# A three-layer graph kernel on one core: the self edge taken out of the gathered edge lists

## The chip, the cores and the metric

The kernel runs on one core of a Trainium2 chip. The metric is the device time of one launch in microseconds, lower is better. PE is TensorE, DVE is VectorE, ACT is ScalarE, POOL is GpSimd, SP is SyncE.

## The reference, cut to what matters

The graph has n = 3125 nodes with D = 128 features, 103125 directed edges sorted by destination, 16 edge types (R), 4 attention heads (H) of 32 features (DH), and L = 3 layers. Two sets of 50000 edges are drawn, and behind them one edge from every node to itself; the sort by destination is stable.

```
_loop = jnp.arange(3125)
src = jnp.concatenate([_s, _d, _loop]); dst = jnp.concatenate([_d, _s, _loop])
_o = jnp.argsort(dst, stable=True); src = src[_o]; dst = dst[_o]
for l in range(3):
    ht = einsum('nd,rdo->nro', h, W_rel[l]);  msg = ht[src, etype]
    h_rel = segment_sum(msg, dst) + h @ W_loop[l] + b_rel[l]
    z = (h @ W_gat[l]).reshape(n, H, DH)
    e = leaky_relu(sum(z*attn_l)[src] + sum(z*attn_r)[dst], 0.2)
    alpha = softmax of e over the edges of one dst
    h_gat = segment_sum(alpha * z[src], dst) + b_gat[l]
    hc = concat([h_rel, h_gat]) @ W_fuse + b_fuse
    if l == 0: hc = hc * sigmoid(concat([hc, mean(weights)]) @ W_gate + b_gate)
    h = relu(hc)
out = layernorm(x + h)
```

So the last edge of every node's list is its edge to itself, with an edge type of its own.

## The kernel before, in words

**Table.** For each layer a table in HBM holds one row of 260 floats for every (node, edge type): 128 of the relation message and 132 of the attention (4 heads of 32 z and one logit). A padded list entry points at a null row (NULL) with a logit of -1e30. Two tables are used in turn.

**Setup.** Degrees are counted with matmuls, every node's edge list (`ell`, up to 80 row numbers) is gathered, nodes are ranked by degree, and POOL scatters (L561) each node's record of start, count, id, x and list in that order; the records come back as `meta`, 25 tiles of 128 nodes. Meanwhile PE, ACT and SP write the first layer's table (L441).

**One layer.** POOL, DVE, ACT and PE each run a loop over the 25 tiles of falling degree. POOL issues an indirect DMA (L594, `fetch`) per list position: 128 rows of 1040 bytes, one for each node. The number of positions of a tile is the largest degree in it (tile 0 is split in two half lists). They come in groups of 16 (PAIR): `H` first, into a buffer in the room of `meta_nat`, then `M1` (buffer in `late`) when there are 32 or more, and the rest, n mod 16, as the tail `T` (buffer in `scratch`). Read off the trace, the tiles have 29, 45, 42, 40, 39, 38, 37, 36, 36, 35, 35, 34, 33, 33, 32, 32, 31, 30, 30, 29, 28, 27, 26, 25 and 23 positions: 825 gathers in a layer. Tiles 1 to 15 have an M1 group, and all but 14 and 15 have a tail.

**What orders it.** Before H POOL waits for the list positions staged by DVE (`stage_head`) and for DVE to have finished the last H group (`free`); M1 and T have `stage_mid` and `stage_tail` likewise. `stage_tail` of a tile is written by `stage_this_tail` (L1344) at the start of that tile on DVE, behind two memsets of the tail buffer (L1334, L1335), and so behind the tail group and `end_tile` of the tile before. In layers 0 and 1 POOL also stores, after H of tile t, the finished table rows of tile t-2 for the next layer (L671, one scatter of 2 MB).

**DVE per tile.** `group` (L1346 on) adds the logits (`raw`, L1353), keeps a running maximum and rescales, sums messages (L1371), weights z by the exponentials that ACT makes (L788 to L1377), and sums (L1381). After the H group comes `epilogue` of the tile before: in layer 0 the gate, in layer 2 the norm. `end_tile` divides and hands `hr`, `hg` to PE (L1025), which transposes and fuses them; the result `hT` is multiplied by all 16 relation weights (L1049) for the next layer's rows, and ACT copies these into `rows` (`next_rows`, L816, L742, L819) and the next er and loop terms (h @ W_loop) into `meta`. At a layer's end POOL stores the last two tiles and waits for them before the first gather of the next (`s_stored`).

## Time and profile before, and how to read it

| | |
|---|---|
| median of 3 runs | 3485.82 us (3484.82 to 3485.93) |
| profiled execution: its span, first to last instruction | 3490.2 us (3490.178) |
| first layer's gathers | 214.5 to 1279 us |
| second layer's gathers | 1315.7 to 2381 us |
| third layer's gathers | 2411.8 to 3451.5 us |
| results stored | 3451.8 to 3484 us |
| POOL busy | 2489.3 us, 71% |
| DVE busy | 2380.3 us, 68% |

No separate time of the profiled execution is shown; its span alone is 4.4 us (0.13%) above the median of the runs. A busy share counts an instruction's own time; the gap between two gathers is called "issue", time in which the engine waited for nothing that the profile shows. A row of the timeline gives start, duration, engine, line and tile names, and in brackets the idle time before it and what ended that.

### The profile page before, as it was taken

Reading aid. Unit: us, or ns where it says so; the run is one execution under the profiler, and the core shown is the slowest. Engines: PE = TensorE matmul, PEld = TensorE weight load, DVE = VectorE, ACT = ScalarE, POOL = GpSimd, SP = SyncE. Lnnn points to the kernel's source line nnn. Section 1 sums busy time; section 2 is a strip of 40 time slices with the busy share of each in tenths; the row PEclk is TensorE's granted clock in tenths of the full one; section 3 lists DMA queues with packets and bytes.
Section 4 is the critical chain, followed back from the end, with each engine's and each line's share of the span. In section 5 each row is a group of like instructions: output and inputs, shape, how many; then the busy total and the mean of one; then the engine's idle time right before and its main releaser. Section 6 shows DMA issues by size and latency. Waiting matters only on the chain.

```text
span 3490.2 us, 18122 instructions
## 1 busy us (share of the span) xinstructions
PE 689.4 (20%) x1897; PEld 372.5 (11%) x1897; DVE 2380.3 (68%) x3226; ACT 424.8 (12%) x769; POOL 2489.3 (71%) x2642
## 2 busy tenths in 40 slices
PE   8942111222122230011121111221000000000000
PEld 5421000111011110000000000110000000000000
DVE  8536666677676764665777756674776788877786
ACT  3530110111111120101111111111000000000000
POOL 1457777777777756777777777775777777777776
PEclk9965555555655555555555555555555555555555
DMA  7774444455545544444454544454433333333332
GB/s 271 315 249 129 134 147 152 152 151 152 152 152 159 168 145 118 130 151 152 151 152 151 153 152 152 152 173 140 107 106 107 107 106 107 106 106 107 106 103 74
DMA packets 143244, 505.96 MB, mean 145 GB/s; under 512 B 44277, under 2 KB 51002, under 8 KB 133618
## 3 DMA queue, kind: packets, MB, share of 16 engines
q0 software_dynamic: 130032, 444.45, 43.4%
q1 hardware_dynamic: 13186, 61.24, 4.5%
q14 instruction: 19, 0.16, 0.0%
q8 instruction: 7, 0.11, 0.0%
HBM read 341.05 MB, written 164.51 MB: 145 GB/s over the span
## 4 chain that ended last, share of the span: by engine, by line
POOL 45%; issue 29%; DVE 10%; DMA 6%; PE 4%; POOLq 3%; DVEq 1%; ACT 1%; SPq 1%; ACTq 0%
POOL meta_nat L594 20%; POOL late L594 14%; POOL scratch L594 10%; DVE acc L1381 3%; PE ps_table L886 1%; DMA late<-table,stage_mid 1%; DMA table<-rows 1%; DMA scratch<-table,stage_tail 1%; DVE late L1377 1%; DVE scratch L1377 1%; DVE meta_nat L1377 1%; POOLq L369 1%; POOL table L671 1%; DMA meta_nat<-table,stage_head 1%; PE ps_cnt L919 1%
## 5 line engine op out<-in xcount | busy, mean ns | idle before, releaser
L594 POOL DMA_INDIRECT meta_nat<-table,stage_head x1200 | 1139.0, 949 | 395.7 <-issue 385.3
L594 POOL DMA_INDIRECT late<-table,stage_mid x720 | 681.9, 947 | 219.4 <-issue 217.9
L594 POOL DMA_INDIRECT scratch<-table,stage_tail x555 | 525.9, 948 | 175.5 <-issue 175.2
L1025 PE MATMUL ps_mix<-ident,hr 128*128 128x128 f32 x75 | 35.5, 473 | 1991.2 <-DVE hg L1401 1991.2
L788 ACT ACTIVATE ps_cnt<-logit 128x68 f32<-128x68 f32 x189 | 43.7, 231 | 2767.1 <-DVE logit L1363 2766.1
L1381 DVE TENSOR_REDUCE acc<-meta_nat 128x132 f32<-128x2112 f32 x75 | 290.6, 3875 | 8.1 <-DVE meta_nat L1377 0.5
L1371 DVE TENSOR_REDUCE acc<-meta_nat 128x128 f32<-128x2048 f32 x75 | 282.6, 3767 | 0.0
L1049 PE MATMUL ps_table<-wrel,hT 128*128 128x512 f32 x400 | 266.4, 828 | 0.0
L1353 DVE TENSOR_TENSOR raw<-late,er_cur 128x64 f32<-128x64 f32 x45 | 12.0, 267 | 324.5 <-DMA late<-table,stage_mid 324.5
L1025 PEld LDWEIGHTS ps_mix<-ident,hr 128*128 128x128 f32 x75 | 13.6, 182 | 2039.8 <-DVE hg L1401 2039.8
L1381 DVE TENSOR_REDUCE acc<-scratch 128x132 f32<-128x1188 f32 (+1 forms) x69 | 208.7, 3024 | 7.1
L1353 DVE TENSOR_TENSOR raw<-meta_nat,er_cur 128x64 f32<-128x64 f32 x75 | 20.1, 267 | 281.6 <-DMA meta_nat<-table,stage_head 280.2
L1371 DVE TENSOR_REDUCE acc<-scratch 128x128 f32<-128x1152 f32 (+1 forms) x69 | 204.9, 2970 | 8.8
L1381 DVE TENSOR_REDUCE acc<-late 128x132 f32<-128x2244 f32 x45 | 183.3, 4072 | 4.7
L1371 DVE TENSOR_REDUCE acc<-late 128x128 f32<-128x2176 f32 x45 | 178.2, 3961 | 5.5
L1334 DVE MEMSET scratch<- 128x1024 f32 (+1 forms) x75 | 93.0, 1240 | 125.5 <-issue 125.5
L1377 DVE TENSOR_TENSOR meta_nat<-meta_nat,ps_cnt 128x2112 f32<-128x2112 f32 x75 | 175.8, 2344 | 3.1 <-ACT ps_cnt L788 3.1
L742 ACT ACTIVATE rows<-ps_table 128x1024 f32<-128x1024 f32 x150 | 148.8, 1026 | 100.2 <-PE ps_table L886 62.4
L1049 PEld LDWEIGHTS ps_table<-wrel,hT 128*128 128x128 f32 x400 | 115.3, 288 | 136.6 <-issue 126.3
L1377 DVE TENSOR_TENSOR scratch<-scratch,ps_cnt 128x1188 f32<-128x1188 f32 (+1 forms) x69 | 127.2, 1843 | 0.0
L1377 DVE TENSOR_TENSOR late<-late,ps_cnt 128x2244 f32<-128x2244 f32 x45 | 111.7, 2482 | 0.0
L1031 PE MATMUL ps_mix<-hrT,wfuse 128*128 128x128 f32 x100 | 39.8, 501 | 363.6 <-ACT hgT L794 363.6
(237 smaller groups left out, 1701.4 us busy)
## 6 DMA issues: line engine op xcount, KB each, us to landing
table<-rows SPq DMA_DIRECT2D x25, 2080.0 KB, 7.7
meta_nat<-table,stage_head POOLq DMA_INDIRECT x1200, 2.8
late<-table,stage_mid POOLq DMA_INDIRECT x720
scratch<-table,stage_tail POOLq DMA_INDIRECT x555, 2.8
meta<-meta_ranked SPq DMA_DIRECT2D x1, 2438.0 KB, 15.1
wrel<-in_L_gnn_W_rel POOLq DMA_DIRECT2D x2, 1024.0 KB, 13.5
meta_nat<-in_x SPq DMA_DIRECT2D x1, 832.0 KB, 18.4
table<-rows,stage_id POOLq DMA_INDIRECT x50, 7.8
```

The costliest lines, as they stand in the source:

```text
L369: n = eng.value_load(tile_slots[0:1, bass.ds(t, 1)], min_val=PAIR, max_val=E)
L594: pool.indirect_dma_start(out=slots[b][:, k, :], out_offset=None, in_=table[l % 2], in_offset=bass.IndirectOffsetOnAxis(ap=index, axis=0)) ...
L671: pool.indirect_dma_start(out=table[(l + 1) % 2][0:NP_ * R, :].rearrange("(n r) f -> n (r f)", r=R), out_offset=bass.IndirectOffsetOnAxis( ...
L742: return s.activation(rows[k][:, j * R // 2:(j + 1) * R // 2, 0:D], ps_table[:, 1024 * j:1024 * j + 1024].rearrange("p (r f) -> p r f", f= ...
L788: s.activation(wgt[:, :, :, 0], logit[:], ACT.Exp).then_inc(s_wgt, 1)
L1025: pe.transpose(mix[0], hr[:], ident[:])
L1031: pe.matmul(mix[2], wfuse[:, 0], hrT[:], start=True, stop=False)
L1049: mm = pe.matmul(ps_table[:, 512 * c:512 * c + 512], hT[0][:], wrel[:, l + 1, c * RC * D:(c + 1) * RC * D], start=True, stop=True)
L1334: v.memset(messages("T", 1, slots_of_tail + 1), 0.0)
L1371: v.tensor_reduce(acc[:, 0:D], messages(b, lo, K + 1).rearrange("p k d -> p d k"), AX.X, ALU.add).then_inc(s_part, 1)
L1377: v.tensor_tensor(weighted(b, lo, K + 1), weighted(b, lo, K + 1), wgt[:, lo:K + 1].to_broadcast([P, K + 1 - lo, H, EX]), ALU.mult).then_in ...
L1381: v.tensor_reduce(acc[:, D:ROW], slots[b][:, lo:K + 1, D:ROW].rearrange("p k f -> p f k"), AX.X, ALU.add).then_inc(s_acc, 1)
```

## The change

Every node of tiles 1 to 24 (rank 128 and up) whose last edge is its own loses that list entry, and its count falls by one. The self edge's logit and z need no gather: in layers 1 and 2, ACT keeps each tile's z in `own_z` (in the room of `rows[1]`) when it writes the rows, and `start_tile` copies it into slot 0 of the H buffer, with `no_own` closing it for tile 0 and padding. Its relation message needs the row of its type: once `rows` of a tile stand, DVE multiplies all 16 rows by a one-hot mask of that type (`own_hot`), sums over the types and adds the sum to the loop term of the next layer (`add_own_messages`). The first layer has no such rows on chip, so it gathers the self edges as one more position, into slot 0 of H, for all 25 tiles. H groups take slot 0 in throughout. `yo` moves into the room of `wrel`.

```diff
+        own_z = rows[1][:].rearrange("p r f -> p (r f)")[:, 0:T * (D + H)].rearrange("p (t f) -> p t f", f=D + H)
...
+            def gather_head(l):
+                if l == 0:
+                    pool.indirect_dma_start(
+                        out=slots["H"][:, 0, :], out_offset=None, in_=table[l % 2],
+                        in_offset=bass.IndirectOffsetOnAxis(ap=stage_head[:, 0:1], axis=0)).then_inc(s_own_landed, 16)
+                gather(l, "H", stage_head[:, 1:PAIR + 1])
...
@@ ACT, next_rows and tile
                     act.wait_ge(s_stored, n_stored)
                     act.reg_add(n_stored, n_stored, 16)
+                    act.wait_ge(s_own_rows, n_own)
...
+                    s.activation(own_z[:, bass.ds(t, 1), :], ps_z[:, 0:D + H].rearrange("p (o f) -> p o f", o=1), ACT.Copy)
...
                 with act.If(groups > 1):
                     group()
-                    with act.If(groups > 2):
-                        group()
                 if not first:
                     next_rows(l, act.snap(n_last, min_val=0, max_val=T - 1))
                     act.reg_add(n_last, n_last, 1)
+                with act.If(groups > 2):
+                    group()
@@ DVE, setup
+            v.tensor_tensor(ell_valid, bc(iota_slot[:], T), bc_last(degree[:], ELL), ALU.is_lt)
+            step(v.tensor_scalar(last_at, degree[:], -1.0, None, ALU.add))
+            v.tensor_scalar(own_at, meta_nat[:, :, M_ID], float(R), 0.5 * (R - 1) - NULL, ALU.mult, ALU.add)
+            step(v.tensor_tensor(is_last, bc(iota_slot[:], T), bc_last(last_at, ELL), ALU.is_equal))
...
+                step(v.tensor_tensor(codes, lists, is_last[:, t0:t1], ALU.mult))
+                step(v.tensor_reduce(code, codes, AX.X, ALU.add))
+                step(v.tensor_tensor(gap, code, own_at[:, t0:t1], ALU.subtract))
+                step(v.tensor_tensor(gone, gap, gap, ALU.mult))
+                step(v.scalar_tensor_tensor(own, gone, 0.25 * R * R, may_drop[:, t0:t1], ALU.is_lt, ALU.mult))
+                step(v.tensor_tensor(gone, code, own, ALU.mult))
+                v.tensor_tensor(codes, is_last[:, t0:t1], bc_last(gone, ELL), ALU.mult)
+                step(v.tensor_tensor(degree[:, t0:t1], degree[:, t0:t1], own, ALU.subtract))
+                v.tensor_scalar(meta_nat[:, t0:t1, M_OWN], gone, float(NULL), None, ALU.add)
+                v.tensor_copy(meta_nat[:, t0:t1, M_CNT], degree[:, t0:t1])
+                v.scalar_tensor_tensor(lists, lists, float(NULL), codes, ALU.add, ALU.subtract).then_inc(s_ell_ok, 1)
@@ DVE, start_tile
+                else:
+                    z = own_z[:, bass.ds(t, 1), :].rearrange("p o (h e) -> p (o h) e", e=EX)
+                    v.tensor_copy(weighted("H", 0, 1)[:, 0, :, 0:DH], z[:, :, 0:DH])
+                    v.tensor_scalar(weighted("H", 0, 1)[:, 0, :, DH], z[:, :, DH], no_own[:, bass.ds(t, 1)], None, ALU.add)
...
+            def add_own_messages(l, t):
+                if l < L - 1:
+                    dve.wait_ge(s_rows, n_rows)
+                    dve.reg_add(n_rows, n_rows, 1)
+                    v.tensor_tensor(own_rows[:], rows[0][:, :, 0:D],
+                                    own_hot[:, bass.ds(t, 1), :].rearrange("p o (r f) -> p (o r) f", f=1
+                                                                           ).to_broadcast([P, R, D]), ALU.mult
+                                    ).then_inc(s_own_rows, 1)
+                    dve.wait_ge(s_own, n_own)
+                    dve.wait_ge(s_own_rows, n_masked)
+                    dve.reg_add(n_masked, n_masked, 1)
+                    v.tensor_reduce(own_sum[:], own_rows[:].rearrange("p r d -> p d r"), AX.X, ALU.add
+                                    ).then_inc(s_own_sum, 1)
+                    dve.wait_ge(s_own_sum, n_own)
+                    dve.reg_add(n_own, n_own, 1)
+                    loop = meta[:, bass.ds(t, 1), M_LOOP:META].rearrange("p o f -> p (o f)")
+                    v.tensor_tensor(loop, loop, own_sum[:], ALU.add).then_inc(s_own, 1)
...
@@ DVE, tile
                 with dve.If(in_first > 1):
                     group("M1")
+                    if not first:
+                        add_own_messages(l, dve.snap(n_last, min_val=0, max_val=T - 1))
...
                 if first:
                     merge_halves(l)
+                else:
+                    if l < L - 1:
+                        with dve.If(in_first < 2):
+                            add_own_messages(l, dve.snap(n_last, min_val=0, max_val=T - 1))
+                    dve.reg_add(n_last, n_last, 1)
                 end_tile(t)
```

Two places of the order of instructions. First DVE in the tile loop of layer 0, from the end of a short tail group (8 positions) to `hg`, the end of the tile. Before:

```order
L1381 TENSOR_REDUCE acc<-scratch 128x132
L1383 REGISTER_ALU
L1509 UNCONDITIONAL_BRANCH
L1396 RECIPROCAL rden<-acc 128x4
L1397 ISA
L1397 TENSOR_TENSOR hr<-acc,meta 128x128
```

Now:

```order
L1439 TENSOR_REDUCE acc<-scratch 128x132
L1441 REGISTER_ALU
L1596 UNCONDITIONAL_BRANCH
L1602 COMPARE_AND_BRANCH
L1475 ISA
L1476 TENSOR_TENSOR own_rows<-rows,own_hot 128x2048
L1482 REGISTER_ALU
L1483 TENSOR_REDUCE own_sum<-own_rows 128x128
L1486 ISA
L1488 TENSOR_TENSOR meta<-meta,own_sum 128x128
L1602 UNCONDITIONAL_BRANCH
L1458 RECIPROCAL rden<-acc 128x4
```

Three operations stand between the tail group's last sum and the end of the tile, for tiles without an M1 group; with one, the same three stand right behind the M1 group instead. Second ACT in the tile loop of layer 1, from the second group's exponentials to the rows of the tile before (`logit` to `ps_cnt` are the exponentials of one group). Before:

```order
L836 COMPARE_AND_BRANCH
L788 ACTIVATE ps_cnt<-logit 128x68
L789 REGISTER_ALU
L838 COMPARE_AND_BRANCH
L788 ACTIVATE ps_cnt<-logit 128x68
L789 REGISTER_ALU
L838 UNCONDITIONAL_BRANCH
L814 REGISTER_ALU
L816 ACTIVATE rows<-ps_z 128x16x132
```

Now:

```order
L868 COMPARE_AND_BRANCH
L816 ACTIVATE ps_cnt<-logit 128x68
L817 REGISTER_ALU
L868 UNCONDITIONAL_BRANCH
L842 REGISTER_ALU
L844 REGISTER_ALU
L846 ACTIVATE rows<-ps_z 128x16x132
L770 ACTIVATE rows<-ps_table 128x8x128 x2
L849 ISA
L849 ACTIVATE rows<-ps_z 128x132
```

The rows of the tile before are now made ahead of the third group's exponentials, and the copy into `own_z` follows them.

## Rows read from the trace of the kernel before

**Rows 1.** Page, part 1: busy time and share of each engine.
```profile
PE 689.4 (20%) x1897; PEld 372.5 (11%) x1897; DVE 2380.3 (68%) x3226; ACT 424.8 (12%) x769; POOL 2489.3 (71%) x2642
```
**Rows 2.** Groups by line: the gathers, busy and mean, idle before and its releasers.
```profile
L594 POOL DMA_INDIRECT meta_nat<-table,stage_head x1200 | 1139.0, 949 | 395.7 <-issue 385.3 <-DVE acc L1381 4.7 <-DVE stage_tail L1344 4.3
L594 POOL DMA_INDIRECT late<-table,stage_mid x720 | 681.9, 947 | 219.4 <-issue 217.9 <-DVE acc L1381 1.5
L594 POOL DMA_INDIRECT scratch<-table,stage_tail x555 | 525.9, 948 | 175.5 <-issue 175.2 <-DVE acc L1381 0.3
```
**Rows 3.** Timeline of POOL, second layer: last tail gather, store, next tail.
```profile
2246.51 0.95 POOL L594 DMA_INDIRECT scratch<-table,stage_tail  x1 [0.30 <-issue]
...
2267.81 1.00 POOL L671 DMA_INDIRECT table<-rows,stage_id  x1 [0.30 <-issue]
2269.11 0.97 POOL L594 DMA_INDIRECT scratch<-table,stage_tail  x1 [0.31 <-issue]
```
**Rows 4.** Timeline of DVE, second layer: a tail group, staging, a shorter tail's memset.
```profile
2249.37 0.26 DVE L1353 TENSOR_TENSOR raw<-scratch,er_cur 128x60 f32<-128x60 f32 x1 [4.75 <-DMA scratch<-table,stage_tail]
...
2257.13 3.86 DVE L1381 TENSOR_REDUCE acc<-scratch 128x132 f32<-128x2112 f32 x1
...
2265.06 0.13 DVE L1344 CAST stage_tail<-meta 128x15 uint32 x1
...
2365.36 0.91 DVE L1334 MEMSET scratch<- 128x1024 f32 x1 [1.70 <-issue]
```
**Rows 5.** Timeline of DVE and POOL, third layer: tail staged, tail gathers started.
```profile
3338.04 0.13 DVE L1344 CAST stage_tail<-meta 128x15 uint32 x1
...
3339.66 0.94 POOL L594 DMA_INDIRECT scratch<-table,stage_tail  x1 [1.16 <-issue]
...
3409.47 0.94 POOL L594 DMA_INDIRECT scratch<-table,stage_tail  x1 [2.40 <-issue]
```
**Rows 6.** Groups by line: operations nearest to the added ones on DVE.
```profile
L1371 DVE TENSOR_REDUCE acc<-meta_nat 128x128 f32<-128x2048 f32 x75 | 282.6, 3767 | 0.0
L1377 DVE TENSOR_TENSOR meta_nat<-meta_nat,ps_cnt 128x2112 f32<-128x2112 f32 x75 | 175.8, 2344 | 3.1 <-ACT ps_cnt L788 3.1
L1397 DVE TENSOR_TENSOR hr<-acc,meta 128x128 f32<-128x128 f32 x75 | 22.1, 295 | 0.2 <-issue 0.2
```
**Rows 7.** Timeline of DVE in the setup: a reduction over adjacent elements.
```profile
144.52 0.69 DVE L1206 TENSOR_REDUCE rank<-scratch 128x4 f32<-128x512 f32 x1
```
**Rows 8.** Timeline of DVE and POOL in the setup: tensor_tensor beside indirect DMAs.
```profile
113.69 2.23 DVE L1174 TENSOR_TENSOR late<-iota_slot,degree 128x2000 bf16<-128x2000 f32 x1
...
114.85 1.92 POOL L549 DMA_INDIRECT meta_nat<-edge_rows,start_u  x1 [0.30 <-issue]
...
159.24 0.81 DVE L1270 TENSOR_TENSOR scratch<-scratch,degree 128x625 f32<-128x625 f32 x1
159.45 1.44 POOL L561 DMA_INDIRECT meta_ranked<-meta_nat,rank_u  x1 [0.30 <-issue]
```
**Rows 9.** Timeline of DVE and POOL, first layer: an M1 group and the next gather.
```profile
786.42 0.27 DVE L1353 TENSOR_TENSOR raw<-late,er_cur 128x64 f32<-128x64 f32 x1 [9.33 <-DMA late<-table,stage_mid]
...
794.54 4.07 DVE L1381 TENSOR_REDUCE acc<-late 128x132 f32<-128x2244 f32 x1
...
798.56 0.97 POOL L594 DMA_INDIRECT meta_nat<-table,stage_head  x1 [0.30 <-issue]
```
**Rows 10.** Timeline of DVE and POOL, end of the second layer.
```profile
2389.07 2.26 DVE L1381 TENSOR_REDUCE acc<-scratch 128x132 f32<-128x1188 f32 x1
...
2411.80 0.98 POOL L594 DMA_INDIRECT meta_nat<-table,stage_head  x1 [7.90 <-issue]
```
**Rows 11.** Timeline of DVE and POOL: start of the first layer.
```profile
207.46 0.17 DVE L1298 CAST stage_head<-meta 128x16 uint32<-128x16 f32 x1
...
214.45 0.95 POOL L594 DMA_INDIRECT meta_nat<-table,stage_head  x1 [11.28 <-issue]
...
251.61 0.94 POOL L594 DMA_INDIRECT meta_nat<-table,stage_head  x1 [1.16 <-DVE acc L1381]
```

More of the change, by code:

```diff
@@ L21 @@
 LEAST = -1.0e37
+SHUT = -1.0e34
 SLOPE = 0.2
@@ L121, in gnn_kernel @@
         rows = [sb(f"rows{i}", [P, R, ROW]) for i in range(2)]
+        own_z = rows[1][:].rearrange("p r f -> p (r f)")[:, 0:T * (D + H)].rearrange("p (t f) -> p t f", f=D + H)
+        assert T <= R * ROW // (D + H)
+        own_type = sb("own_type", [P, T])
+        own_hot = sb("own_hot", [P, T, R])
+        no_own = sb("no_own", [P, T])
+        own_sum = sb("own_sum", [P, D])
+        own_rows = sb("own_rows", [P, R, D])
+        own_room = own_rows[:].rearrange("p r d -> p (r d)")
+        is_last = own_room[:, 0:T * ELL // 2].bitcast(BF16).rearrange("p (t j) -> p t j", t=T)
+        last_at, own_at, apart, may_drop, last_code, is_own, dropped = (
+            own_room[:, T * ELL // 2 + i * T:T * ELL // 2 + (i + 1) * T] for i in range(7))
+        assert T * ELL // 2 + 7 * T <= R * D
         degree = sb("degree", [P, T])
@@ L686, in tile @@
                 free("H")
-                gather(l, "H", stage_head)
+                gather_head(l)
                 if l < L - 1:
@@ L1344, in stage_this_tail, with group @@
                 v.tensor_copy(stage_tail[:], meta_flat[:, bass.ds(at, PAIR - 1)]).then_inc(s_tail, 1)
-            def group(b, first=False, meanwhile=None, K=PAIR):
-                lo = 1 if first else 0
+            def group(b, first=False, meanwhile=None, K=PAIR, own_gathered=False):
+                lo = 1 if first and not own_gathered else 0
+                new = 0 if first else 1
                 dve.wait_ge(s_landed[b], n_land[b])
@@ L1376, in group @@
                 dve.wait_ge(s_wgt, n_g)
-                v.tensor_tensor(weighted(b, lo, K + 1), weighted(b, lo, K + 1),
-                                wgt[:, lo:K + 1].to_broadcast([P, K + 1 - lo, H, EX]), ALU.mult).then_inc(s_product, 1)
+                v.tensor_tensor(weighted(b, 0, K + 1), weighted(b, 0, K + 1),
+                                wgt[:, 0:K + 1].to_broadcast([P, K + 1, H, EX]), ALU.mult).then_inc(s_product, 1)
                 dve.wait_ge(s_part, n_g)
                 dve.wait_ge(s_product, n_g)
-                v.tensor_reduce(acc[:, D:ROW], slots[b][:, lo:K + 1, D:ROW].rearrange("p k f -> p f k"), AX.X, ALU.add
+                v.tensor_reduce(acc[:, D:ROW], slots[b][:, 0:K + 1, D:ROW].rearrange("p k f -> p f k"), AX.X, ALU.add
                                 ).then_inc(s_acc, 1)
```

71 lines of the change are left out of this document (47 added, 24 removed).

## The prediction

> **What bounds the kernel now.** I read the busy shares first, then the groups by line, then the timeline of POOL beside DVE. The shares decide nothing: POOL 71%, DVE 68% [rows 1]. The groups do: 2475 gathers are 2346.8 us busy, mean 0.948, and the 790.6 us idle before them are 778.4 us "issue"; DVE's `acc` and `stage_tail` together end only 10.8 us of it [rows 2]. So POOL issues one gather after another, every 3137 / 2475 = 1.27 us, stalls included, and about 1.25 us where none stalls, and whoever takes a gather away gains 1.25 us, as long as DVE does not come to hold POOL back. The timeline tells how far it is from that. With m tail gathers in a tile, POOL's way from one tail to the next is m + 16 gathers and a store: 1.25(m+16) + 1.30 = 1.25m + 21.3 us in the second layer; with m = 12, of which row one is the last, 2246.51 to 2269.11 is 22.6 us, that is 17 gathers and the store, whose place takes 1.30 [rows 3]. DVE has a way of its own between the same two points, through the staging of the tail: last tail gather to the group's start 2.86 us, the group 11.62 us (2249.37 to 2260.99), from there to `stage_tail` written 4.20 us [rows 4], and 1.49 us until POOL starts [rows 5]. From the first tail gather that is 1.25(m-1) + 20.17 = 1.25m + 18.9. The slack of POOL over DVE is 2.4 us per tile. In the third layer, without the store and with the norm on DVE, it is used up in the last tiles: waits of 1.16 and 2.40 us where 0.30 is usual [rows 5]; five such tiles make some 7 us.
>
> **The gathers.** The reference puts a self edge last in every list, so each of tiles 1 to 24 loses one position: that the lists stay as long is excluded. Second and third layer lose 24 gathers each, 30.0 us each. The first layer trades 24 for 24 and adds one in tile 0. There POOL waited 1.16 us before tile 1 [rows 11], so 0.4 us remain.
>
> **What DVE gets, `own`.** Per tile of layers 0 and 1: the mask, 2048 elements, 2.33 us (2112 take 2.344 [rows 6]); the sum of 16 rows into 128, a strided read of 2048 elements exactly as L1371, 3.77 us [rows 6]; the add 0.295 [rows 6]; and about 0.1 between. That is **6.5 us**. Bounds: if the sum ran at the rate of adjacent elements, 0.69 us for 512 [rows 7], it would be 2.3 us and own 5.0; above, if the other stride costs more or the branches show, I take 7.2. I take 6.5, since L1371 has the same shape. All 50 are 325 us of DVE, most of it in its idle time.
>
> **Tail loop.** In tiles 14 to 24 (one full group now) own stands between the tail group and `end_tile`, so in front of the next `stage_tail`. DVE's way becomes 1.25m + 25.4, longer than POOL's 1.25m + 21.3 (first layer, with its H gather more, 22.6). POOL waits 4.1 us per tile in the second layer, 2.8 in the first. Tiles 15 to 22 pay this in full. Tile 14 comes behind an M1 group of 12.19 us (786.42 to 798.61 [rows 9]): from its last gather DVE needs 2.86 + 12.19 + 6.5 + 4.20 + 1.49 = 27.2, POOL 17 gathers and the store, 22.6, so 4.6 and 3.4. Behind tile 22 the memset is for 8 positions, 1024 elements in 0.91 us [rows 4], 0.8 less than for 1920 at that rate, and with what the H buffer takes already tile 23 waits 3.0 and 2.0. Behind tile 23 the tail group itself is for 8 positions, and no wait is left. Sum: 8 x 4.1 + 4.6 + 3.0 = 40.4 and 8 x 2.8 + 5.4 = 27.8 us. The H buffer adds some 2 us in the second layer, where the H gathers of tiles 13 and 24 wait for an H group that now ends later.
>
> **The mask against the gathers.** This is what the diff doesn't show. An indirect DMA that starts while DVE is in a tensor_tensor with both inputs in SBUF does not run: L1174 ends at 115.92 and the L549 begun at 114.85 takes 1.92 instead of 0.95, ending 0.85 us behind it; L1270 ends at 160.05, and the L561 begun at 159.45 ends at 160.89 [rows 8]. The mask is such an operation, 2.33 us long. Where it follows the M1 group it starts at about 798.53, and the next gather at 798.56 [rows 9]; the distance repeats, because the landing of the last gather starts the group. So a gather is held through all of it, **2.2 us** for each of 13 tiles in two layers. In the tiles with one group the loss falls into the wait for `stage_tail`; about 3 of the 26 do so too. 23 x 2.2 = 51 us, and some 9 us more in the last two tiles of both layers, whose masks hold gathers too and where the shorter waits no longer take that in: 60. Bounds: 0, and 2.33 each.
>
> The Trainium skill, "SBUF — State Buffer", section "Who interferes with whom", infers that a tensor_tensor takes only the read side of the port pair shared with GpSimd, while descriptor generation needs the write side, and so does not stall it. By it this term is 0. The trace contradicts it with the 1.92 us, so I go by the row and keep the rule as a rival.
>
> **Layer ends.** POOL waits there for the last rows; from DVE's last sum, 2391.33, to the next gather are 20.5 us [rows 10]. Own of tile 23 stands in front of `end_tile` of tile 24: 6.5 us, plus 0.3 for the ACT copy of z, and 1 to 1.5 for rows that are not yet there behind a short tail and longer H groups. 8.3 in the first layer, 7.7 in the second. The own of tile 24 lies beside the next layer's first gathers (20 us).
>
> **Small edits.** Slot 0 in H groups 0.3 to 0.5 us and two copies in `start_tile` 0.45 us: hidden by the slack except in the third layer's last tiles, where waits grow from 7 to 11 us, with the shorter tails. Reordering ACT: nothing, the third exponential waits for DVE anyway. Setup: about 4.5 us per list chunk on DVE; the first chunk is in front of POOL's scatters, which lead to `stage_head` at 207.63 and the first gather at 214.45 [rows 11]. 4.6 of nearly 7 us are used, and masks there hold a few scatters: 2 us, between 0 and 6.
>
> **Sum.**
>
> | | us |
> |---|---|
> | first layer: 0.4 + 27.8 + 8.3 | +36.5 |
> | second: -30.0 + 40.4 + 2 + 7.7 | +20.1 |
> | third: -30.0 + 4 | -26 |
> | gathers held by masks | +60 |
> | setup | +2 |
> | sum | +92.6 |
>
> Against its own span, 3490.2, this gives 3582.8; the median lay 4.4 below that span, so I forecast 3485.8 + 92 = **3578**.
>
> **Rivals.**
> - Gathers are not held (the rule above), the loops bind: +32.6, 3518. For it: the two cases stand in the setup, with other targets. Against: the same kind of index read from SBUF. 0.16.
> - They are held half, because a gather begun 0.03 us from the mask's start may get in first and only the one after it is caught, 1.25 us into the mask: 1.1 us each, so half of the 60, +62, 3548. 0.16.
> - The other side: the sum runs at the adjacent rate or faster, and nothing is held. Each microsecond of own costs 22 (two layers of ten tiles, and their ends), so the loops and ends balance the saved gathers at own = 5.0 us: 3486, no change, 0.05. Below that it gains; at own = 4, 3468. The rows put a floor of 5.0 under own, so this takes a DVE way that has more slack than I read: if the tail is not waited for at all, 60 saved less 22 is 3448. 0.08.
> - Own of 7.2 us or more, with the gathers held: 0.7 x 22 more at most, 3592 and above. 0.05.
>
> My forecast has the rest, 0.50. Slower are 0.50 + 0.16 + 0.16 + 0.05 = 0.87, the same 0.05, faster 0.08. The range takes in the slower cases and the bounds of setup and own, 3510 to 3602. 0.2% are 7 us, about what a measurement of this kernel can tell from no change.
>
> **What would show it.** The mask at 2.3 us, the sum at 3.8; gathers of 3.1 us, one for each mask behind an M1 group; waits of POOL for the tail of some 2 to 4 us in tiles 14 to 23 of the first two layers and none before; the third layer some 26 us shorter, from first to last gather 1040 to 1014; first layer longer by over 50. I am wrong if L594's longest stays near 1.07 us, or if the first layer's gathers take no longer than before.

## The result and the profile after

| | before | changed kernel |
|---|---|---|
| median of 4 runs | 3485.32 us (3483.24 to 3485.93) | 3563.38 us (3560.76 to 3565.3) |
| profiled execution, span | 3490.2 us | 3563.6 us |
| first gather of the first layer | 214.45 | 219.01 |
| from there to the second layer's first | 1101.25 | 1159.55 |
| second layer's to the third's | 1096.10 | 1134.76 |
| third layer's to the first result stored | 1040.0 | 1014.01 |
| POOL busy, DVE busy | 71%, 68% | 70%, 75% |

The ratio is 1.0223, 95% interval 1.021 to 1.0235: 78 us slower. The forecast was 3578 us, range 3510 to 3602. The spans differ by less, 73.4 us: that of the kernel before is 4.4 us above its median, that of the changed kernel only 0.2 us. By stages the 73.4 are +4.6 in the setup, +58.3 and +38.7 in the first two layers, -26.0 in the third, -2 behind it. These rows of POOL's timeline bound the stages of the changed kernel (start, duration, engine, line, operation and names, idle time before it):

```profile
219.01 0.95 POOL L625 DMA_INDIRECT meta_nat<-table,stage_head  x1 [8.14 <-DVE stage_head L1344]
...
1378.56 0.98 POOL L614 DMA_INDIRECT meta_nat<-table,stage_head  x1 [7.89 <-issue]
...
2513.32 0.98 POOL L614 DMA_INDIRECT meta_nat<-table,stage_head  x1 [8.63 <-issue]
...
3527.33 1.03 POOL L707 DMA_INDIRECT out<-wrel,id_u  x1 [0.30 <-issue]
```

The costliest groups by line, of the same profile (busy us, mean ns of one | idle before, and what ended it), answer to [rows 2]:

```profile
L614 POOL DMA_INDIRECT meta_nat<-table,stage_head x1200 | 1195.0, 996 | 390.5 <-issue 368.3
L614 POOL DMA_INDIRECT late<-table,stage_mid x624 | 591.7, 948 | 190.1 <-issue 187.4
L614 POOL DMA_INDIRECT scratch<-table,stage_tail x579 | 547.8, 946 | 226.0 <-issue 223.8
...
L1483 DVE TENSOR_REDUCE own_sum<-own_rows 128x128 f32<-128x2048 f32 x50 | 178.9, 3578 | 9.4 <-DVE own_rows L1476 9.3
...
L1476 DVE TENSOR_TENSOR own_rows<-rows,own_hot 128x2048 f32<-128x2048 f32 x50 | 114.2, 2283 | 18.2 <-ACT meta L850 18.2
```

Two things stand in them. The idle time before the tail gathers of `scratch` is 226 us for 579, 0.39 each, where 0.30 is the least: POOL waits in front of some. And the gathers into `meta_nat` have a mean of 996 ns, where those into `late` keep 948. It isn't that all of them became a little slower. One line's instructions (minimum, median and maximum in ns) show a few very long ones:

```profile
L614 POOL DMA_INDIRECT meta_nat<-table,stage_head x1200: 942/946/3078, 220.3 to 3518.6; - x172
```

The long ones lie beside the mask. In POOL's and DVE's timeline behind the M1 group of tile 1 in the first layer, and behind that of tile 9:

```profile
311.63 0.95 POOL L614 DMA_INDIRECT scratch<-table,stage_tail  x1 [0.30 <-issue]
311.71 2.27 DVE L1476 TENSOR_TENSOR own_rows<-rows,own_hot 128x2048 f32<-128x2048 f32 x1
312.88 1.93 POOL L625 DMA_INDIRECT meta_nat<-table,stage_head  x1 [0.31 <-issue]
314.18 3.58 DVE L1483 TENSOR_REDUCE own_sum<-own_rows 128x128 f32<-128x2048 f32 x1 [0.19 <-DVE own_rows L1476]
...
721.54 2.28 DVE L1476 TENSOR_TENSOR own_rows<-rows,own_hot 128x2048 f32<-128x2048 f32 x1
721.59 3.05 POOL L614 DMA_INDIRECT meta_nat<-table,stage_head  x1 [0.30 <-issue]
```

The mask starts 0.08 us after a gather has begun, and that gather passes. The next one begins 1.17 us into the mask and is held, that is, it lasts longer than the usual 0.95 us: the mask ends at 313.98, the gather at 314.81, 0.83 later, 0.98 us over the usual length. Only where a gather begins just after the mask (721.59 against 721.54) is it held for the whole of it, 2.1 us. Of the 50 masks 49 hold a gather, together 65 us, and all 49 held gathers end 0.81 to 0.87 us after their mask. (Three of the 49 are stores of table rows at the ends of the layers; they are the same kind of indirect DMA.)

The other loss is the wait for the tail. In tile 16 of the second layer:

```profile
2144.22 0.99 POOL L699 DMA_INDIRECT table<-rows,stage_id  x1 [0.30 <-issue]
2145.85 1.66 DVE L1388 MEMSET scratch<- 128x1920 f32 x1 [1.77 <-issue]
2147.50 0.13 DVE L1398 CAST stage_tail<-meta 128x15 uint32 x1
2149.10 0.96 POOL L614 DMA_INDIRECT scratch<-table,stage_tail  x1 [3.89 <-issue]
```

POOL has issued its store by 2145.21 and stands until 2149.10, since `stage_tail` is written only at 2147.63. In [rows 3] the same wait was 0.31. The reading "issue" hides it: no instruction of another engine that the profile shows ends the wait, so the idle time has to be set against 0.30.

### The profile page after: what moved, and what is told of

Its sections match the earlier page's. It is cut to its first block, busy times and chain, and to the rows that moved or that the text cites. A ratio compares the mean times of both kernels' runs of the same rounds, so it can differ in the third digit from the quotient of the medians.

```text
span 3563.6 us, 18787 instructions
## 1 busy us (share of the span) xinstructions
PE 685.9 (19%) x1897; PEld 369.1 (10%) x1897; DVE 2690.2 (75%) x3453; ACT 431.6 (12%) x813; POOL 2508.9 (70%) x2595
## 4 chain that ended last, share of the span: by engine, by line
POOL 37%; issue 31%; DVE 17%; DMA 7%; PE 4%; POOLq 2%; DVEq 1%; SPq 1%; ACT 1%; ACTq 0%
POOL meta_nat L614 16%; POOL late L614 13%; POOL scratch L614 6%; DVE own_sum L1483 3%; DVE acc L1439 3%; DMA late<-table,stage_mid 3%; DVE late L1435 2%; DMA meta_nat<-table,stage_head 2%; DVE own_rows L1476 2%; PE ps_table L918 1%; DVE meta_nat L1435 1%; DMA scratch<-table,stage_tail 1%; DVE scratch L1435 1%; PE ps_cnt L951 1%; POOLq L389 1%
## 5 line engine op out<-in xcount | busy, mean ns | idle before, releaser
L614 POOL DMA_INDIRECT late<-table,stage_mid x624 | 591.7, 948 | 190.1 <-issue 187.4
L1439 DVE TENSOR_REDUCE acc<-meta_nat 128x132 f32<-128x2244 f32 x75 | 306.6, 4088 | 7.7
L1429 DVE TENSOR_REDUCE acc<-meta_nat 128x128 f32<-128x2048 f32 (+1 forms) x75 | 288.2, 3843 | 0.0
L1439 DVE TENSOR_REDUCE acc<-scratch 128x132 f32<-128x2112 f32 (+1 forms) x69 | 213.5, 3094 | 7.1
L1429 DVE TENSOR_REDUCE acc<-scratch 128x128 f32<-128x2048 f32 (+1 forms) x69 | 208.9, 3028 | 8.8
L1388 DVE MEMSET scratch<- 128x1920 f32 (+1 forms) x75 | 95.3, 1270 | 135.7 <-issue 135.7
L1483 DVE TENSOR_REDUCE own_sum<-own_rows 128x128 f32<-128x2048 f32 x50 | 178.9, 3578 | 9.4 <-DVE own_rows L1476 9.3
L1435 DVE TENSOR_TENSOR meta_nat<-meta_nat,ps_cnt 128x2244 f32<-128x2244 f32 x75 | 185.9, 2478 | 0.0
L1435 DVE TENSOR_TENSOR scratch<-scratch,ps_cnt 128x2112 f32<-128x2112 f32 (+1 forms) x69 | 130.2, 1887 | 0.0
L1476 DVE TENSOR_TENSOR own_rows<-rows,own_hot 128x2048 f32<-128x2048 f32 x50 | 114.2, 2283 | 18.2 <-ACT meta L850 18.2
## 6 DMA issues: line engine op xcount, KB each, us to landing
wrel<-in_L_gnn_W_rel POOLq DMA_DIRECT2D x2, 1024.0 KB, 13.3
```

The lines of the kernel that those rows point to most:

```text
L614: pool.indirect_dma_start(out=slots[b][:, k, :], out_offset=None, in_=table[l % 2], in_offset=bass.IndirectOffsetOnAxis(ap=index, axis=0)) ...
L1388: v.memset(messages("T", 1, slots_of_tail + 1), 0.0)
L1429: v.tensor_reduce(acc[:, 0:D], messages(b, lo, K + 1).rearrange("p k d -> p d k"), AX.X, ALU.add).then_inc(s_part, 1)
L1435: v.tensor_tensor(weighted(b, 0, K + 1), weighted(b, 0, K + 1), wgt[:, 0:K + 1].to_broadcast([P, K + 1, H, EX]), ALU.mult).then_inc(s_prod ...
L1439: v.tensor_reduce(acc[:, D:ROW], slots[b][:, 0:K + 1, D:ROW].rearrange("p k f -> p f k"), AX.X, ALU.add).then_inc(s_acc, 1)
L1476: v.tensor_tensor(own_rows[:], rows[0][:, :, 0:D], own_hot[:, bass.ds(t, 1), :].rearrange("p o (r f) -> p (o r) f", f=1).to_broadcast([P, ...
```

## The experiments

**What the reader must know first.** In all of the experiments the kernel before took 3962 to 3972 us (medians of 7 to 19 runs), not 3485. It was so on all four occasions, on chips 4, 2 and 9; on which chip the first pair ran isn't on record, and the kernel before wasn't profiled again. For the changed kernel there is a profile of either level. The gathers last as long in both and DVE's operations within 0.5% in sum, but DVE stands far longer between them, at the starts of tiles above all. The rows of the register and branch instructions show what it does there (experiment 7); why it does so stays open. So no experiment repeats the +78 us, and none gives the price of a part under the conditions of the forecast. What they do show is what a gather beside a mask does, which doesn't hang on it, and what becomes of the change when DVE's way through a tile is longer than POOL's nearly everywhere: in the later profile of the changed kernel POOL waits over 0.5 us in 64 of the 72 tiles (three layers, without tile 0), in the first in 27. All ratios are to the kernel before, timed beside each kernel, with 95% intervals.

Two theories were on trial. "Own" is the mask, the sum over types and the addition on DVE. The first theory: own makes the whole loss, by holding gathers while the mask reads two SBUF operands, and by standing in front of `stage_tail`. The other: a hold comes from the mask's place or length, or costs nothing, or other parts of the change cost too.

**1. The mask's weights in PSUM.**

```diff
-        own_hot = sb("own_hot", [P, T, R])
+        own_hot = ps_cnt[:, 17 * H:17 * H + T * R].rearrange("p (t r) -> p t r", r=R)
```

> The changed kernel with one thing altered: the 25x16 one-hot weights of the mask lie in PSUM, in the bank that holds the exponentials, so the mask multiplies an SBUF operand by a PSUM one, as the weighting product of a group does. Theory (the mask holds the gather that is issued while it runs because both its operands are in SBUF): gathers no longer last 1.9 to 3.1 us next to a mask, the 36 + 30 us that the first and second layers' gathers last over 0.95 us go to under 2 us. Of these, 28 us (26 masks behind an M1 group at about 1.07) come off the time; the other 38 us lie in the tiles of one group, where POOL then waits for the staged tail instead, up to the 68 us that the recurrence had for those waits (41.6 us are measured now): about 11 us off. Time 3524, range 3515 to 3540. Rival 1 (the mask holds gathers wherever its weights lie): 3563. Rival 2 (each hold is paid in full, no wait takes its place): 3497.

Measured 3985.8 us, ratio 1.0056 (1.0037 to 1.0075).

> hot_psum once more. If the kernel before takes about 3485 here: 3524 (3515 to 3540) by the theory, 3497 if each hold was paid in full, 3563 if holds cost nothing. If about 3970: 3986 as before, ratio 1.006, and 20 to 66 us under the changed kernel beside it.

Measured 3993.33 us, ratio 1.0063 (1.0037 to 1.0089). Of 50 masks none holds a gather, in either run, though 78 gathers begin inside a mask in each; they last 0.94 to 0.99 us. The timeline of the second run, behind the M1 group of tile 1 as above:

```profile
343.08 0.95 POOL L615 DMA_INDIRECT scratch<-table,stage_tail  x1 [0.30 <-issue]
343.15 2.29 DVE L1477 TENSOR_TENSOR own_rows<-rows,ps_cnt 128x2048 f32<-128x2048 f32 x1
344.33 0.95 POOL L626 DMA_INDIRECT meta_nat<-table,stage_head  x1 [0.30 <-issue]
345.58 0.95 POOL L615 DMA_INDIRECT meta_nat<-table,stage_head  x1 [0.30 <-issue]
```

And the durations of this line's instructions in the same run:

```profile
L615 POOL DMA_INDIRECT meta_nat<-table,stage_head x1200: 940/946/1075, 228.1 to 3937.8; - x172
```

The mask is as long (2.29 us), as far from the gather before it (0.07), and only the place of one operand differs; the longest gather into `meta_nat` falls from 3057 ns in the unaltered changed kernel timed beside it (experiment 5) to 1075. So it is the second SBUF operand that holds them, not the mask's length or its place. The rival "wherever its weights lie" is out as to the mechanism. The expected 20 to 66 us were not gained. The kernel even took 20 us more than the unaltered one beside it (3993.33 against 3973.63), and POOL's waits before head gathers are 213 us in the first two layers in place of 168: where DVE's way is the longer one, the freed gathers only wait elsewhere. Where the 20 us come from isn't shown.

The Trainium skill, "SBUF — State Buffer", section "Who interferes with whom", states both sides of this: a DVE instruction with at most one SBUF input, outside of the 2-port modes, doesn't contend with GpSimd, and one with two contends with a GpSimd instruction that reads SBUF. These traces agree, with 49 of 50 against 0 of 50 in each of six runs with the weights in PSUM. Its inference that a tensor_tensor therefore leaves descriptor generation alone doesn't hold for an indirect DMA: the 49 of the first profile are held for 0.5 to 2.1 us each.

**2. The mask computed twice**, back to back, same output.

```diff
+                    v.tensor_tensor(own_rows[:], rows[0][:, :, 0:D], own_hot[...], ALU.mult).then_inc(s_once, 1)
+                    dve.wait_ge(s_once, n_once)
+                    dve.reg_add(n_once, n_once, 1)
                     v.tensor_tensor(own_rows[:], rows[0][:, :, 0:D], own_hot[...], ALU.mult
                                     ).then_inc(s_own_rows, 1)
```

> The changed kernel with the mask computed twice, the second behind the first's end (a wait of about 0.2 us between), weights in SBUF; same output. Theory (a gather that begins while a mask runs ends 0.82 us after that mask, whatever its phase: so in all 49 held gathers of the changed kernel): each mask holds its own gather, unless none begins in it. If the gap of 0.2 us lets the first held gather end at 0.82 us into the second mask, a second gather begins 0.3 us later and is held by the rest, about 1.15 us: per pair 0.98 + 1.15 behind an M1 group in place of 0.98. If the gap is too short to write its descriptors, one gather lasts to 0.82 us after the second mask: 0.98 + 2.47 = 3.45 us over. Summed over the first two layers about 65 us become 120 (gap used) or 185 (not used). Time beside the kernel before: if that takes about 3485, 3563 + 26 x 1.2 to 2.5 + 20 x 2.5 = 3644 to 3678; if about 3970, 3974 + 50 x 2.47 at most = 3974 to 4097.

Measured 3983.99 us in a single run, beside 3962.24; this difference has no interval. Behind the M1 group of tile 1:

```profile
342.33 0.94 POOL L615 DMA_INDIRECT scratch<-table,stage_tail  x1 [0.30 <-issue]
342.43 2.27 DVE L1478 TENSOR_TENSOR own_rows<-rows,own_hot 128x2048 f32<-128x2048 f32 x1
343.58 1.94 POOL L626 DMA_INDIRECT meta_nat<-table,stage_head  x1 [0.30 <-issue]
344.82 2.29 DVE L1484 TENSOR_TENSOR own_rows<-rows,own_hot 128x2048 f32<-128x2048 f32 x1
345.82 2.11 POOL L615 DMA_INDIRECT meta_nat<-table,stage_head  x1 [0.30 <-issue]
```

The first gather ends at 345.52, 0.82 after the first mask and 0.70 into the second: the gap between the masks, 0.12 us, lets it through, and its last 0.7 us run beside a mask unhindered. The second one is held again, to 0.82 after the second mask. That is the "gap used" case: 94 of the 100 masks hold a gather, 121 us in the first two layers, as expected. A gather is caught at one moment near its beginning, not throughout, which fits that one begun 0.07 us ahead of the mask passes.

**3. Own later.** Own of tile t-2 runs behind the H group and epilogue of tile t, in all tiles.

```diff
                 if not first:
                     epilogue(l, dve.snap(n_last, min_val=0, max_val=T - 1))
+                    if l < L - 1:
+                        with dve.If(t > 1):
+                            add_own_messages(l, dve.snap(n_two_ago, min_val=0, max_val=T - 1))
+                            dve.reg_add(n_two_ago, n_two_ago, 1)
...
-                        with dve.If(in_first < 2):
-                            add_own_messages(l, dve.snap(n_last, min_val=0, max_val=T - 1))
```

> The changed kernel with own's three operations of tile t-2 run behind the H group and epilogue of tile t in every tile, instead of those of tile t-1 at the end of tile t (one group) or behind its M1 group. Weights still in SBUF. Theory (own stands ahead of the staging of the next tail, and POOL waits for it): POOL's waits for stage_tail in tiles 14 to 24 of the first two layers fall from 14.7 + 26.9 us to under 8 in all, and some 10 us of the layer ends go too, since the last tile but one's own no longer stands ahead of the last tile's end; the masks still hold gathers (48 of 0.9 to 2.3 us). Time 3515, range 3490 to 3540. Rival 1 (the wait only moves: own now delays the T group and with it the next staging, as DVE's own work of a tile, about 30 us, bounds it): 3550 to 3563, waits for stage_tail as before. Rival 2 (where a mask lies decides nothing): same 66 us over for the held gathers.

Measured 4005.22 us, ratio 1.0098 (1.007 to 1.0125). 42 masks hold gathers, 65.1 us in all, which end 0.81 to 0.86 us after the mask; now gathers into `late` and `scratch` are among them, at most 2981 and 2904 ns. So where a mask lies chooses the victim, not the loss. POOL's waits before the first tail gather of a tile, over the usual 0.30, sum to 45 and 56 us in the first two layers, more than the 14.7 and 26.9 of the changed kernel's first profile and in sum about the 51 and 52 of the unaltered kernel in experiment 5: where DVE's way is the longer one, the wait isn't removed by a move on DVE. This kernel ran on one occasion only, and whether the move pays where POOL's way is the longer one it can't tell.

**4. Both together.**

> hot_psum and own_later together. Theory: neither holds nor waits for the staged tail are left; what own costs is at most its share where DVE's work of a tile comes near POOL's (tails of 8 slots: DVE about 30 us against POOL's 31.3): 3437 plus up to 15, so 3445, range 3437 to 3465, faster than before (3485) by 0.6 to 1.4 per cent. Rival (own behind the H group delays the T group and the next staging by as much): 3500 or more.

Measured 3990.9 us, ratio 1.0055 (1.0037 to 1.0073).

> both once more (weights in PSUM, own of tile t-2 behind the H group of tile t). If the kernel before takes about 3485: 3445 (3437 to 3465), faster than before by 0.6 to 1.4 per cent, and no more than 15 us over no_own. Rival: the T group is late in place of the staging, 3500 or more. If about 3970: 3991, ratio 1.0055.

Measured 3999.11 us, ratio 1.0085 (1.0054 to 1.0116).

> Weights of the mask in PSUM, own of tile t-2 behind the H group of tile t, on another occasion. If the kernel before takes about 3485 (DVE's tile starts 1.7 us): POOL bounds most tiles, no gather is held, the staged tail is there in time: 3445, range 3437 to 3465, ratio 0.987 to 0.994; rival, the T group is late in its place: 3500 or more. If it takes about 3970 (tile starts up to 13.4 us): DVE bounds, neither the freed gathers nor the place of own is worth anything: 3991 to 3999, ratio 1.006 to 1.0085.

Measured 3986.53 us, ratio 1.0058 (1.0029 to 1.0088). In the second of these three runs the unaltered changed kernel was timed beside it, and this one took 25 us more. No version with the full output beat the kernel before. The version expected at 3445 never ran under the conditions that this number was for, so that number is neither shown nor refuted.

**5. The changed kernel once more**, as a yardstick.

> The changed kernel, unaltered, as the yardstick of this call: the kernel before took 3969.55 us beside the last four kernels and not 3485, with the same durations of single instructions, but up to 13.4 us without an instruction on DVE at a tile's start (1.7 in the profile of the kernel before). If the kernel before takes about 3485 here: 3563, gathers of the first two layers 36 + 30 us over 0.95 us each. If it takes about 3970 again: DVE, not POOL, bounds the tiles there, own's 6.4 us are paid in most of 48 tiles and the third layer's 26 us are worth less: 3913.6 (no_own) + 48 x 2 to 48 x 6.4, so 4010 to 4200; ratio 1.01 to 1.05.

Measured 3973.63 us beside 3968.44, ratio 1.0017 (0.9995 to 1.0038): here the change makes no difference that can be told, where it was 1.0223 ahead of it. The gathers were expected to be held as before, and they are, 67 us. POOL's waits are far longer: 51 and 52 us before the first tail gathers of the two layers, and 91 and 77 before the first head gathers (the layer's first left out), where the first profile has 4.2 and 3.3. DVE's way is the longer one, as expected, but the price of own was put too high: at least 4010 was expected. One start of a tile in this run's timeline:

```profile
543.54 0.29 DVE L1463 TENSOR_TENSOR hg<-acc,rden 128x128 f32<-128x128 f32 x1 [1.11 <-issue]
...
556.42 0.95 POOL L614 DMA_INDIRECT late<-table,stage_mid  x1 [0.30 <-issue]
556.48 0.91 DVE L1388 MEMSET scratch<- 128x1024 f32 x1 [12.65 <-issue]
```

Between `end_tile` and the memset of the next tile stand only branches, a load of the tile's count into a register and register work. They took about 1.7 us (median) in both profiles ahead of the experiments and 12.65 here, while POOL issues gathers at its usual distance.

**6. No own.** Mask, sum and addition left out, so the output lacks the messages of the dropped self edges in the second and third layers; the rest of the change stays.

```diff
             def add_own_messages(l, t):
-                if l < L - 1:
...
+                pass
```

> The changed kernel without own's mask, sum and addition (ACT doesn't wait for the mask either), so the output lacks the message of each dropped self edge in the second and third layers; everything else of the change stays. Theory (own alone makes the loss, by held gathers, tail waits and layer ends): first layer 1101 us from first gather to the next layer's, second 1066, third 1014, setup 4.6 later than before: 3563 - 58 - 69 = about 3437, range 3430 to 3445. Rival (other parts of the change cost too: the copy of z on ACT, next_rows ahead of the third group, the two copies into slot 0, the 17th gather): layers longer than this, 3450 or more.

Measured 3913.6 us, ratio 0.9868 (0.9842 to 0.9894).

> no_own once more (no mask, sum and addition; the output lacks the dropped self edges' messages in the second and third layers). If the kernel before takes about 3485: 3437 (3430 to 3445) if own alone makes the loss, 3450 or more if other parts of the change cost too. If about 3970: 3914, ratio 0.987.

Measured 3911.75 us, ratio 0.988 (0.9843 to 0.9917), and 61.9 us under the unaltered kernel timed beside it (3973.63). So the change without own gains 56.7 us over before (3968.44), and own gives all of it back. The 56.7 are near the 51 that the forecast's terms for gathers and third layer come to with the measured setup (60 less 0.4, less 4, less 4.6), which speaks against other parts of the change costing much. It doesn't prove it, since a microsecond of either engine isn't worth a microsecond here.

Own is 305 us of DVE's busy time, yet it costs 62. DVE's wait list says where the rest went; its row for the memset that begins a tile gives the idle time before it in us, the times, and the longest. In the first profile of the changed kernel:

```profile
DVE scratch L1388 <- issue: 135.7, 75, 2.8
```

In after_again:

```profile
DVE scratch L1388 <- issue: 348.4, 75, 13.3
```

In no_own_again, where the line is L1386:

```profile
DVE scratch L1386 <- issue: 475.9, 75, 13.4
```

In mask_twice, where it is L1389:

```profile
DVE scratch L1389 <- issue: 257.3, 75, 13.4
```

With own left out, DVE is busy 2395.8 us instead of 2701.1, and 127.5 us come back at the tile starts. With the mask doubled it is busy 2813.0, and 91.1 us go from there (on another occasion and chip). Under these conditions DVE's busy time is worth only a part of itself, in either direction.

**7. Is it the length of DVE's code?** The theory was that DVE stands at the starts of tiles because its loop is too long to stay loaded. The code for a tile's third and later groups, which these inputs never reach (no tile has over 45 slots), left out of DVE's program.

```diff
                 with dve.If(in_first > 1):
                     group("M1")
...
-                    with dve.If(in_first > 2):
-                        group("M2")
...
```

> The changed kernel with the code for a tile's third and later groups (M2, the second M1 and the loop over further blocks) left out of DVE's program: no tile of these inputs has more than 45 slots, so it never runs, and the output is the same; DVE's code between a tile's start and end is about a third shorter. Kernels took 3962 to 3970 (before) in all runs of this study but 3485 ahead of the prediction, with DVE idle up to 13.4 us at a tile's start. Theory (DVE waits there for code of its own loop, since the loop is too long to stay loaded): tile starts of about 1.7 us again, POOL bounds again: about 3563 as ahead of the prediction, gathers held for 36 + 30 us, POOL's waits for stage_tail 42 us. Partly short enough: between 3600 and 3900. Rival (the stall is not one of code length): 3974 as without the cut, tile starts up to 13.4 us.

Measured 3995.3 us, ratio 1.0052 (1.0035 to 1.0068). The same row of its wait list:

```profile
DVE scratch L1388 <- issue: 392.6, 75, 14.1
```

> The same cut in the kernel with the weights in PSUM and own of tile t-2 behind the H group of tile t. If DVE's tile starts are 1.7 us again: 3445 (3437 to 3465), that is 100 to 125 us below after_lean, by 66 us of holds and 42 us of waits for the staged tail, and some 10 us at the layer ends. Rival 1 (own delays the T group instead): 3500 to 3563. Rival 2 (stalls as before the cut): 3987 to 3999, no better than after_lean.

Measured 4007.04 us, ratio 1.0093 (1.0076 to 1.011). The tile starts are no shorter, 392.6 us against 348.4: this theory fell.

What DVE does in these times stands in the rows of its register and branch instructions, which the timeline leaves out. Between the rows at 543.54 and 556.48 above there are eight of them, a load into a register and a check of the loaded value, all but one 0.70 or 0.71 us long and begun 0.7 or 1.4 us apart. Two lines of `kernel.py` show both levels: the loop over the tiles (L1616) and `norm_step` in the third layer (L1517), a wait and one register addition between two operations of the norm, with no branch. Count, then duration in ns (minimum, median, maximum) and first and last start; first profile of the changed kernel:

```profile
L1616 DVEq COMPARE_BRANCH  x72: 50/56/63, 330.8 to 3546.7; - x72
L1517 DVEq ALU_OP  x350: 40/40/40, 2584.2 to 3554.9; - x175
```

after_again:

```profile
L1616 DVEq COMPARE_BRANCH  x72: 13/63/1397, 358.6 to 3977.3; - x72
L1517 DVEq ALU_OP  x350: 3/40/709, 2824.4 to 3982.6; - x175
```

And what it does to the norm, three operations on one element each per partition, in after_again; in the first profile the same three stand 0.12 to 0.13 us apart:

```profile
3621.95 0.15 DVE L1554 TENSOR_SCALAR newton<-newton_i 128x1 int32<-128x1 int32 x1 [1.25 <-issue]
3623.36 0.27 DVE L1530 TENSOR_SCALAR newton<-newton,ve 128x1 f32<-128x1 f32 x1 [1.25 <-issue]
3624.75 0.15 DVE L1531 TENSOR_SCALAR newton<-newton 128x1 f32<-128x1 f32 x1 [1.12 <-issue]
```

Behind 215 us DVE runs 2855 register and branch instructions in the changed kernel. In the first profile the longest lasts 0.22 us; in after_again 683 last over 0.4 us, most of these 0.70. POOL has it too, 372 of 2086, and so have all twelve profiles of the experiments; those of the kernel before and of the changed kernel ahead of them have none on either engine. On DVE there are 923 in no_own_again, where DVE has less to do, and 460 in mask_twice, where it has more, which fits the idle time that came back and went in experiment 6. after_lean has 697. So the lost time isn't one of tile starts or of branches alone, and a shorter loop on DVE doesn't take it away.

The Trainium skill, "Runtime: NRT & Kernel Launch", section "Instruction fetch mechanics", says that a taken branch to code outside the two pages that are loaded costs a DMA fetch. No run here shows such a fetch: DVE's register instructions are long without a branch too, as in the norm, and the DMA rows of after_again from 534 to 566 us list packets of the gathers' queue alone. (Packets of instruction queues stand elsewhere in that trace; it doesn't say for which engines they are recorded.) What makes them 0.70 us long stays open.

## Why the prediction was right, term by term

The direction was right and the time inside its range, 15 us under the forecast. Its terms can all be read off the first pair of profiles. In this table "waits" are POOL's idle times over 0.30 us before the first tail gather of a tile, "held" is what a gather lasts over 0.95, and a layer end is the time from the end of a layer's last gather to the next layer's first, over that of the kernel before and less what its stores are held.

| term | forecast | measured |
|---|---|---|
| own per tile | 6.5 | 6.43 (mask 2.28, sum 3.58, add 0.29, the rest between them) |
| gathers fewer | -29.6, and -30.0 in the third layer | the same counts of 25, 24 and 24 |
| tiles 14 to 23, second layer | 40.4 | 26.9 waits + 14.5 held = 41.4 |
| the same, first layer | 27.8 | 14.7 + 16.0 = 30.7 |
| H buffer, second layer | 2 | 1.7 |
| H buffer, first layer | nothing | 2.7 (0.87 and 3.19 us before tiles 23 and 24, less 0.10 and 1.23 before the change) |
| masks behind an M1 group | 51 | 30.1 |
| masks in the last two tiles | 9 | 4.0 |
| layer ends | 8.3 + 7.7 | 6.7 + 10.1 |
| third layer | -26 | -26.0 |
| setup | +2 | +4.6 |

- **What bounds the kernel:** right. POOL's cadence is 1.25 us still, and DVE's way, 6.4 us longer, is now the longer one in tiles of one group.
- **Own:** right in its sum, partly by luck. The forecast had the sum over types as long as L1371, 3.77 us, and it took 3.58; the mask was put at 2.33, where [rows 6] scale to 2.27; the time between the three operations, put at 0.1, is some 0.3. The lower bound was misread: 0.69 us for 512 elements [rows 7] are 2.8 us for 2048, not 2.3, so by the rows own could not go below 5.5, and the rivals of no change and of a gain had less behind them than their 0.05 and 0.08.
- **Tail loop:** right within 4 us in 68, in its sum. It was forecast as waits of 4.1 and 2.8 us alone; in fact a mask there holds a gather and the wait shrinks by as much (in the second layer 3.9 us of idle time where 1.36 are held, 2.6 where 1.4 to 1.7 are). DVE's way decides the sum, and it doesn't matter how POOL spends it.
- **The mask against the gathers:** this is the step that failed, in its size. The text put the mask's start at 798.53 and the next gather at 798.56, "so a gather is held through all of it, 2.2 us". The mechanism was right; the order of the two was not. The mask starts 0.03 to 0.23 us behind a gather's begin in 21 of these 26 tiles, that gather passes, and the next is caught some 1.1 us in; in the first layer mostly 1.17: 2.28 + 0.82 - 1.17 - 0.95 = 0.98. These 21 held 0.94 to 1.15 us, and all 26 in sum 30.1 in place of 51. This was the rival "held half", at 0.16: the gather that gets in first was its own reason, and its 1.1 us the right size. Its time, 3548, lies as far below the result as the forecast above it, for the gathers held were 34.1 in place of its 30, tail loop and setup came out 6.5 higher, and H buffer and layer ends 3.2. The distance was guessed to 0.03 us from two durations, each with a rounding of that size; a choice between 1.0 and 2.2 us can't rest on that, and half the chance on each side would have been honest.
- **H buffer in the first layer:** a term that was put at nothing without a reason. H of tile 24 waits 3.19 us over the usual for the H group of tile 23, 1.96 more than before the change: one tail gather fewer lies between (1.25 us), and the group's three large operations are together 0.56 us longer with slot 0 (3.98, 2.48 and 4.07 us, where they were 3.77, 2.34 and 3.86). The forecast had such waits in the second layer alone.
- **Layer ends, third layer:** 16.8 against 16.0, -26.0 against -26. The second agrees in part by luck: POOL's waits there grew by 5.7 us and not 4, before the H gathers of tiles 23 and 24 (6.0 us), not before tails, and the gathers were 2 ns shorter on average, 1.6 us in all.
- **Setup:** 4.6 against 2, inside its bounds of 0 and 6. The 8.14 us before the first gather say that POOL waited for `stage_head` on DVE.

The measured terms sum to 76.4 us, where the stages up to the first result stored give 75.5 (and 73.4 with the 2.1 less behind it). Not in the table are a second wait of 1.9 us within the tail of tile 17 in the second layer, and gathers that, where not held, were 1.4 to 1.7 ns shorter on average in the first two layers, 2.5 us in all. The forecast had 92.6: 20.9 too much in the masks behind M1 groups and 5.0 in those of the last two tiles, against 3.9 too little in the tail loop, 2.6 in the setup, 2.4 in the H buffer and 0.8 at the layer ends. So 9.7 of the 25.9 us too much were made up by terms that were too small; without that luck the forecast would have been some 24 us too high and not 15. The medians lie 4.6 us further apart than the spans.

**What stays open.** The prices of hold and wait under the first conditions: the terms add up, but no run there took one of them away, so this is argued and not shown. And why register instructions of 0.04 to 0.2 us take 0.70 in the later profiles, and whether that alone makes the kernel before take 3970 us in place of 3485, since it was not profiled again.

## What to carry to other kernels

A tensor_tensor of DVE with two SBUF operands, 2.28 us long, beside a stream of indirect DMAs on POOL held the first one that began inside it until 0.82 us after it; with one operand in PSUM it held none, at the same length. The place of the rest of DVE's work counts too: work on a staging path costs what it adds beyond the slack, whatever the mean busy shares are. And when a kernel's time hangs on which of two engines is ahead, a change may cost 2.2% at one time and nothing that can be told at another: time both kernels together, each time, and where a kernel's time has moved, look at the durations of its register instructions as well.

## What the runs showed of the hardware that was not expected

- A gather needs what the mask withholds only at one early moment: begun 0.03 to 0.09 us ahead of a mask it runs 0.95; begun inside it ends 0.81 to 0.87 after it, in five profiles and 283 cases; and its last 0.7 us run beside a second mask unhindered.
- The stream of gathers can fix the phase, since the landing of the last gather starts the group: in the first profile 21 of the 26 masks behind an M1 group came 0.03 to 0.23 us behind the begin of a gather and held the next for 0.94 to 1.15 us. In after_again, where DVE stood for changing times, only 11 of the 26 did, and the 49 held gathers lost 1.38 us each in place of 1.32. So the sum of the holds is much the same, 67 and 65 us.
- DVE's branches and register work between two tiles took 1.4 to 2.8 us in all 75 tile starts of the first profile of the changed kernel, and 1.5 to 13.3 in the 75 of the later one. The busy time of DVE was the same within 0.5%, 2690.2 and 2701.1 us: the 425.6 us between the two spans are time without an operation, not longer operations.
- In that time the register and branch instructions themselves last 0.70 us in place of 0.04 to 0.2, on DVE and on POOL, with a branch or without, in 683 of DVE's 2855. The setup, up to 215 us, has none of them.
